# Attention block on one core: projection split four and four around the first row maxima, weights and gate product placed later

## Chip, cores, metric

The kernel runs on one core of one Trainium2 chip. The metric is the device time of one execution, in microseconds (us). TensorE is PE in the profile, VectorE DVE, ScalarE ACT, GpSimd POOL, and SyncE SP; SP only issues the DMAs here, one after the other.

## The reference, cut to what matters

The input is 2 batches of 2048 tokens with 256 features. Four residual layers follow each other: grouped attention, a feed-forward net that is applied three times, a linear attention with a gate, and the feed-forward net again. The change concerns the start of the first layer, and small pieces of the two that follow.

```python
x = x + attn_a(layernorm(x), Wq, bq, Wk, bk, Wv, bv, Wo, bo)   # 16 heads of 16, 4 KV heads
    q, k, v = x @ Wq + bq, x @ Wk + bk, x @ Wv + bv
    out = softmax(q k^T / sqrt(16)) v ;  out @ Wo + bo
x = x + ffn(layernorm(x), ...)
x = x + attn_b(layernorm(x), ...)       # gate = sigmoid(x @ Wg1 @ Wg2)
x = x + ffn(layernorm(x), ...)
```

## The kernel before

**Projection.** The 4096 tokens are 8 chunks of 512; chunks 0 to 3 are batch 0. For each chunk DVE takes moments (`moments_of`), POOL the root (`root`, a power on 4 columns), DVE scales (`scaled`), PE turns the rows (`turn_rows`), ACT copies them to `YT` (`put_row`), and PE projects: three groups of heads (`project_heads`, n = 0, 1, 2) and the values (`project_values`). Queries and keys are kept as three bf16 parts that add up to the f32 value: ACT writes the f32 value and part 0 (`high`), then comes `residue` (value minus part 0), ACT's `middle` (part 1) and `low` (part 2). `residue` and `low` are DVE's for chunks below `FREE` = 6 and POOL's for the other two. SP stores each part to DRAM (`store`: three DMAs, keys once and queries twice), and DRAM hands them back in the layout of the scores.

**Buffers of parts.** `part_a` holds two chunks, `part_b` two more; chunks 0 to 3 take turns in `part_a`, chunks 4 to 7 in `part_b`, so chunk c waits for the stores of chunk c-2 (`stored(act, 0, c - 2)`), but for chunks 4 and 5.

**Steps.** The attention is 32 steps (8 KV heads by 4 query chunks). For step s first come 64 row maxima: one bf16 matmul each on PE (`max_mm`, line 675, banks 0 to 2 of PSUM in turn) and one reduction on DVE (line 1488). When all 64 are there, DVE makes the negated maxima and signals `nm_t`; SP then issues `load_negated` (8 DMAs, line 466), and the scores of the step (lines 723 and 729) can be made with the maximum subtracted; the matmul of line 729 waits for it (`m_ld`). ACT takes the exponentials (line 1126), PE the sums with the values (line 700). In the steady state PE makes the maxima of step s+1 among the scores of step s, 16 of them (`AHEAD`) already before the step begins.

**The start.** Step 0's maxima have no scores to go beside. Before the change chunks 0 to 5 are projected, and then chunks 6 and 7 are projected in pieces between the 64 maxima (`BLOCK` = 32 maxima for each chunk). Then PE makes 16 maxima of step 1, `gate_turn` and `gate_product` (Wg1 @ Wg2, into `lvg_s`, with ACT's copies), and enters `step(0, 0)`.

**SP's queue** in order: X chunks and first weights, all 36 other weights (line 426), then the stores of the chunks with loads between them: the queries of steps 0 and 1 for the maxima (`load_queries`) after chunk 0, the keys (`load_keys`) after part 1 of chunk 3, `load_scores` of step 0 (16 coarse and 8 fine DMAs) after chunk 4 and of step 1 after chunk 6. Behind all the stores stands `load_negated(0)`, then `refill_max(0, 0)` (16 DMAs, for step 2's maxima) and the loop of the steps, which begins with `next_maxima(0, 0)`: wait for `nm_t` of step 1, `load_negated(1)`.

**Others.** POOL sets two rows of ones (`kb_ones`), copies the values of steps 0 and 1, makes residue and low of chunks 6 and 7, and adds the output bias to X (`add_bias`, line 1800, 8 instructions); DVE makes twelve small constants from the weights (lines 1450 to 1460) between chunk 5's parts and the first maximum. In `feed_forward(0)` the items n = 0, 1, ... run as a hand-written pipeline of `first(n)`, `second(n-1)`, `third(n-3)`, `fourth(n-4)` on PE, each answered by ACT. `ORDER[6]` to `ORDER[9]` are second cycles, so DVE's `update(n)` stands between PE's `first(n)` and ACT's. `global_net` of batch 1 runs at n = 8, 9, 10 and uses bank 7, as the gate product does.

Of the kernel before, what the change touches and what calls it, by code (L numbers as in the profile page):

```python
# [48 lines left out]
FREE = NCH - 2  # L49
# [21 lines left out]
def hybrid_block(nc, x, wq, bq, wk, bk, wv, bv, wo, bo, lq, lk, lv, lo, g1, g2, ln_w, ln_b,  # L71
                 c1, d1, c2, d2, c3, d3, c4, d4, e1, f1, e2, f2, e3, f3, ar,
                 ident_in, cos_in, sin_in, causal_in, head_in, diag_in, sign_in, out):
    with ExitStack() as ctx:
# [149 lines left out]
        def part(c, pt):  # L224
            return (part_a if c < CPG else part_b)[:, c % 2, pt]
# [105 lines left out]
        def buffer_of(c):  # L331
            return c // CPG * 2 + c % 2

        def stored(eng, pt, c):

            if c >= 0:
                eng.wait_ge(p_st[pt][buffer_of(c)], STORED * (c % CPG // 2 + 1))
                eng.wait_ge(k_st[pt][buffer_of(c)], 16 * (c % CPG // 2 + 1))
# [77 lines left out]
        def _(sp):  # L416
# [8 lines left out]
            for dst, src in weights:  # L425
                sp.dma_start(dst, src).then_inc(w_ld, 16)  # L426

# [52 lines left out]
            for c in range(NCH):  # L480
                store(c, 0, p_act)
                store(c, 1, p_mid)
                if c == CPG - 1:
                    for pt in range(2):
                        for p in range(2):
                            sp.wait_ge(k_st[pt][p], 16 * CPG // 2)
                    load_keys(ka, 0, 0, qa_ld)
                store(c, 2, p_low)
                if c == 0:
                    stored(sp, 0, 0)  # L490
                    stored(sp, 1, 0)
                    for s in (0, 1):
                        load_queries(qa, s, s, qa_ld)
                if c == CPG:
                    load_keys(ka, 1, 1, qa_ld)
                    stored(sp, 2, CPG - 2)
                    stored(sp, 2, CPG - 1)
                    load_scores(0, 0)
                if c == NCH - 2:
                    load_scores(1, 1)  # L500
# [106 lines left out]
        def _(pe):  # L607
# [137 lines left out]
            def gate_turn():  # L745

                pe.wait_ge(n_y, 2 * NCH)
                for kt in range(KT):
                    m = pe.transpose(ps[0:HD, 7, kt * P:(kt + 1) * P], g1_s[:, kt, :], ident[:])
                m.then_inc(w_gt, 1)  # L750

            def gate_product():

                pe.wait_ge(w_ge, 1)
                for kt in range(KT):
                    m = mm(ps[:, 7, kt * DIM:(kt + 1) * DIM], g1_t[:, kt, :], g2_s[:], start=True, stop=True)
                m.then_inc(w_gm, 1)

# [5 lines left out]
            for c in range(FREE, NCH):  # L764
                x = BLOCK * (c - FREE)
                for n in range(3):
# [4 lines left out]
                    if n < KT and c + 1 < NCH:  # L771
                        first_maxima(x, x + 1)
# [3 lines left out]
                        x += 2  # L776
# [4 lines left out]
                first_maxima(*range(x, BLOCK * (c - FREE + 1)))  # L781
            for x in range(AHEAD):
                max_mm(0, 1, x)
            pe.wait_ge(w_ld, 16 * len(weights))
            gate_turn()
            gate_product()
# [4 lines left out]
            pe.wait_ge(w_gs, KT)  # L791
# [13 lines left out]
            def feed_forward(k):  # L805
# [4 lines left out]
                def global_net(layer, b):  # L810
# [11 lines left out]
                    m.then_inc(f_g, 1)  # L822

# [56 lines left out]
                for n in range(LAST + 1):  # L880
# [176 lines left out]
        def _(act):  # L1057
# [11 lines left out]
            def high(c, n):  # L1069

                act.wait_ge(p_mm, 4 * c + n + 1)
                if n == 0:
                    if c not in (CPG, CPG + 1):
                        wait(act, p_low, c - 1)
                        stored(act, 0, c - 2)
# [4 lines left out]
            def middle(c):  # L1080
                act.wait_ge(p_res, c + 1)
                if c not in (CPG, CPG + 1):
                    stored(act, 1, c - 2)
# [18 lines left out]
            for pt in range(3):  # L1102
                for c in (NCH - 2, NCH - 1):
                    stored(act, pt, c)


            act.wait_ge(w_gt, 1)
            act.copy(g1_t[:].rearrange("p k n -> p (k n)"), ps[0:HD, 7, 0:KT * P]).then_inc(w_ge, 1)
            act.wait_ge(w_gm, 1)
            for kt in range(KT):  # L1110
                act.copy(lvg_s[:, kt, DIM:2 * DIM], ps[:, 7, kt * DIM:(kt + 1) * DIM]).then_inc(w_gs, 1)

# [35 lines left out]
            def feed_forward(k):  # L1148
                base, pairs = k * FN, k * FN // 2

                def global_net(layer, b):
# [5 lines left out]
                    if layer == 2:  # L1157
                        fn(gth[:, b:b + 1], ps[:, 7, 0:1], ACT.Tanh, bias=half_b[:, 1:2], scale=0.5).then_inc(f_ga, 1)

# [60 lines left out]
                for n in range(LAST):  # L1220
# [15 lines left out]
                    if n + 2 < NCH:  # L1236
                        put_rows(st, n + 2)

# [124 lines left out]
        def _(dve):  # L1363
# [61 lines left out]
            def low(c):  # L1425
                dve.wait_ge(p_mid, c + 1)
                if c not in (CPG, CPG + 1):
                    stored(dve, 2, c - 2)
# [20 lines left out]
            dve.wait_ge(w_ld, 16 * len(weights))  # L1449
            dve.tensor_scalar(ct_s[:, 0, :], c1_s[:, 1, :], bias[:, SG:SG + 1], -1.0, ALU.mult, ALU.mult).then_inc(c_tw, 1)  # L1450
            dve.tensor_scalar(ct_s[:, 1, :], c1_s[:, 0, :], bias[:, SG:SG + 1], None, ALU.mult).then_inc(c_tw, 1)
            dve.tensor_copy(w4_s[0:64, 0:1], last_c[0:64, 0:1])
            dve.tensor_copy(w4_s[64:P, 1:2], last_c[64:P, 0:1])
            dve.tensor_copy(c4_s[:], last_c[:, 0:1].broadcast_to((P, P))).then_inc(cols, 1)
            dve.tensor_copy(e3_s[:], last_c[0:64, 1:2].broadcast_to((64, P))).then_inc(cols, 2)
            dve.tensor_scalar(half_b[:, 0:1], bias[:, D4:D4 + 1], 0.5, None, ALU.mult)
            dve.tensor_scalar(half_b[:, 1:2], bias[:, F3:F3 + 1], 0.5, None, ALU.mult).then_inc(c_dve, 1)
            dve.memset(coup[:, 2:3], 0.1)
            dve.tensor_scalar(coup[:, 1:2], bias[:, AR:AR + 1], 0.3, None, ALU.mult)
            dve.tensor_scalar(coup[:, 3:4], bias[:, AR:AR + 1], 0.7, None, ALU.mult).then_inc(c_dve, 1)  # L1460

# [22 lines left out]
            def maxima(s, p, before=True):  # L1484
                for x in range(MAXU):
# [3 lines left out]
                    if not before and x % BLOCK == 20:  # L1489
                        put_values(FREE + x // BLOCK)  # L1490
# [10 lines left out]
            maxima(0, 0, before=False)  # L1501
            maxima(1, 1)
# [8 lines left out]
            negated_turn(STEPS - 1)  # L1511

# [267 lines left out]
        def _(pool):  # L1780
# [26 lines left out]
            def low(c):  # L1807
                pool.wait_ge(p_mid, c + 1)
                stored(pool, 2, c - 2)
# [3 lines left out]
            for c in range(NCH):  # L1813
                root(0, c)
            pool.wait_ge(n_rs, NCH)

            for pt in range(3):
                for c in (CPG - 2, CPG - 1):
                    stored(pool, pt, c)
            pool.wait_ge(p_low, CPG)  # L1820
            pool.memset(kc[FINE:FINE_M], 1.0).then_inc(kb_ones, 1)
            pool.memset(kc[HALF + FINE:HALF + FINE_M], 1.0).then_inc(kb_ones, 1)
            pool.wait_ge(kb_ones, 2)
# [5 lines left out]

            pool.wait_ge(p_val, CPG)  # L1830
            values(0, 0)
            values(1, 1)
            for c in range(FREE, NCH):
                residue(c)
                low(c)
            pool.wait_ge(w_ld, 16 * len(weights))
            pool.wait_ge(nm_t, 1)
            for c in range(NCH):
                add_bias(c)
            pool.wait_ge(p_val, NCH)  # L1840
            pool.wait_ge(n_bo, NCH)
# [4 lines left out]

            for c in range(NCH):
# [138 lines left out]
```

## Time and profile before

| | us |
|---|---|
| median of 3 runs | 2129.47 (2126.69 to 2131.73) |
| profiled execution | 2132.38 |
| its span, first to last instruction | 2130.6 |
| PE busy in the span | 2007.4 (94%) |
| DVE busy in the span | 1824.8 (86%) |
| ACT busy in the span | 1488.5 (70%) |

The span is what a trace covers; the execution's own time is a little longer. A busy share is an average over stages that have different limits, so the stages are read one by one: a row of a timeline gives the start, the length, the engine, the line, what is written from what, the count, and in brackets the idle time before it and who ended it.

### The profile page before, as it was taken

What the parts mean: (1) busy time and instruction counts of PE and PEld (TensorE: products, weight loads), DVE (VectorE), ACT (ScalarE), POOL (GpSimd) and SP (SyncE); (2) the same over time, 40 slices, a digit from 0 to 9 for tenths busy, and PEclk for the clock granted to TensorE, in tenths of its full rate; (3) what the DMA queues carried; (4) which work ended last, traced back from release to release, by engine and by line L of the source; (5) the groups of instructions that cost most, each with busy time, mean ns of one, the idle gap of its engine ahead of it and who ended that gap; (6) DMA issues with size and microseconds to landing.
All of it is one profiled execution on the core that took longest, in us unless ns stands there. A gap on an engine that the chain in (4) does not pass through costs nothing.

```text
span 2130.6 us, 47788 instructions
## 1 busy us (share of the span) xinstructions
PE 2007.4 (94%) x13990; PEld 819.3 (38%) x13990; DVE 1824.8 (86%) x3396; ACT 1488.5 (70%) x2939; POOL 178.9 (8%) x298
## 2 busy tenths in 40 slices
PE   7689999999999999999999999989997799998995
PEld 4323333333333333333333333334433466665432
DVE  6789999999999999999999999945449977777358
ACT  4428888888888888888888888854457554444757
POOL 1250000000000000000000000001005211002001
PEclk9769999999999999999999999999998899998998
DMA  6421122122112112112212212222000000000002
GB/s 163 135 75 43 44 64 64 43 58 70 43 53 71 46 47 73 50 45 69 56 43 67 60 42 65 52 88 87 1 1 1 1 1 1 1 0 1 1 1 80
DMA packets 110232, 101.34 MB, mean 48 GB/s; under 512 B 52240, under 2 KB 91424, under 8 KB 110096
## 3 DMA queue, kind: packets, MB, share of 16 engines
q1 hardware_dynamic: 110096, 99.92, 17.6%
q14 instruction: 99, 0.81, 0.1%
q8 instruction: 37, 0.61, 0.1%
HBM read 78.79 MB, written 20.77 MB: 47 GB/s over the span
## 4 chain that ended last, share of the span: by engine, by line
PE 82%; DVE 7%; ACT 4%; issue 3%; SPq 3%; DMA 1%; ACTq 0%; DVEq 0%; POOL 0%; POOLq 0%
PE ps L700 22%; PE ps L675 15%; PE ps L723 10%; PE ps L729 10%; PE ps L840 6%; PE ps L849 3%; PE ps L938 2%; PE ps L947 2%; PE ps L986 2%; PE ps L689 2%; ACT YT L1126 2%; PE ps L967 1%; PE ps L1017 1%; DVE X L1607 1%; SPq L426 1%
## 5 line engine op out<-in xcount | busy, mean ns | idle before, releaser
L1488 DVE TENSOR_REDUCE mx<-ps 128x1 f32<-128x512 f32 x2048 | 1279.8, 683 | 21.1 <-PE ps L675 16.5
L1126 ACT ACTIVATE YT<-ps 128x512 f32<-128x512 f32 x2048 | 1058.2, 605 | 253.0 <-PE ps L729 253.0
L700 PE MATMUL ps<-YT,work 128*32 128x512 f32 x4096 | 546.2, 605 | 0.0
L675 PE MATMUL ps<-work 64*128 64x512 bf16 x2048 | 460.7, 389 | 16.0 <-DVE mx L1488 13.3
L723 PE MATMUL ps<-work 64*128 64x512 bf16 x2048 | 402.5, 378 | 1.7
L729 PE MATMUL ps<-work 34*128 34x512 bf16 x2048 | 398.9, 378 | 0.0
L675 PEld LDWEIGHTS ps<-work 64*128 64x128 bf16 x2048 | 144.6, 93 | 620.8 <-DVE mx L1488 547.0
L723 PEld LDWEIGHTS ps<-work 64*128 64x128 bf16 x2048 | 162.0, 94 | 106.4 <-ACT YT L1126 32.0
L700 PEld LDWEIGHTS ps<-YT,work 128*32 128x32 f32 x4096 | 80.7, 108 | 122.9 <-issue 87.2
L729 PEld LDWEIGHTS ps<-work 34*128 34x128 bf16 x2048 | 101.2, 94 | 49.2 <-issue 1.3
L1827 POOL COPY work<-vals 128x512 f32 (+1 forms) x32 | 19.6, 613 | 1191.9 <-PE ps L700 1191.8
L849 PE MATMUL ps<-work,c_s 128*128 128x512 f32 x192 | 97.1, 630 | 14.5 <-ACT work L1177 12.1
L1688 DVE TENSOR_TENSOR work<-ps,causal 128x512 f32<-128x512 f32 x128 | 81.7, 681 | 22.0 <-PE ps L967 22.0
L840 PE MATMUL ps<-YT,c_s 128*128 128x512 f32 x128 | 62.3, 632 | 5.0 <-ACT vals L1172 2.8
L938 PE MATMUL ps<-lqk_s,work 128*128 128x512 f32 x128 | 63.6, 620 | 3.4 <-DVE work L1706 2.2
L840 PE MATMUL ps<-YT,ct_s 128*128 128x512 f32 x128 | 60.9, 619 | 4.3 <-issue 4.3
L947 PE MATMUL ps<-lvg_s,work 128*128 128x512 f32 x128 | 61.7, 605 | 3.1 <-ACT YT L1062 3.1
L1306 ACT ACTIVATE work<-ps 128x128 f32<-128x128 f32 x64 | 14.2, 274 | 69.2 <-PE ps L947 69.2
L849 PEld LDWEIGHTS ps<-work,c_s 128*128 128x128 f32 x192 | 36.0, 196 | 65.8 <-issue 45.5
L1326 ACT ACTIVATE work<-ps,bias 128x128 f32<-128x128 f32 x64 | 25.8, 454 | 38.1 <-PE ps L1007 38.1
L1672 DVE TENSOR_TENSOR work<-work,cos_s 128x256 f32<-128x256 f32 x64 | 27.0, 422 | 29.2 <-ACT work L1298 29.1
L620 PE MATMUL ps<-ident,xn 128*128 128x128 f32 x256 | 37.3, 292 | 15.6 <-DVE xn L1394 10.8
(178 smaller groups left out, 1809.6 us busy)
## 6 DMA issues: line engine op xcount, KB each, us to landing
work<-k_scr SPq DMA_DIRECT2D x640, 64.0 KB, 2.2
work<-q_scr SPq DMA_DIRECT2D x640, 32.0 KB, 1.8
o_scr<-o_sb SPq DMA_DIRECT2D x32, 256.0 KB, 2.2
X<-in_L_attn_a_x_dram SPq DMA_DIRECT2D x8, 512.0 KB, 7.4
work<-negt SPq DMA_DIRECT2D x256, 1.0 KB
work<-o_scr SPq DMA_DIRECT2D x16, 256.0 KB
work<-inv_scr SPq DMA_DIRECT2D x16, 256.0 KB
out_dram<-X SPq DMA_DIRECT2D x8, 512.0 KB, 2.9
```

The lines of the kernel that those rows point to most:

```text
L675: mm(ps[:, bank_of[x], :], qa[rows, p, jp, qt * P:(qt + 1) * P], ka[rows, p, kc_ * CH:(kc_ + 1) * CH], start=True, stop=True).then_inc(a_m ...
L689: m = mm(ps[:, last_bank(c, h), (t % 2) * DIM:(t % 2 + 1) * DIM], a_in[:, c % 2, kt, t * P:(t + 1) * P], wo_s[:, kt, :], start=kt == 0, st ...
L700: m = mm(ps[32 * j:32 * j + 32, 7, :], vst[:, p, t, :], prob(GROUP * t + j), start=t == 0, stop=t == KTILES - 1)
L723: mm(ps[:, S_BANK + (u + g) % S_RING, :], kb[rows, p, t * P:(t + 1) * P], qb[rows, p, jp, :], start=True, stop=False)
L729: mm(ps[:, S_BANK + (u + g) % S_RING, :], kc[rows, p, t * P:(t + 1) * P], qc[rows, p, jp, :], start=False, stop=True).then_inc(qk_mm, 1)
L840: m = mm(ps[:, b_ + mt, :], w[:, kt, mt * P:(mt + 1) * P], YT[:, kt, ch(c)], start=kt == 0, stop=kt == KT - 1)
L849: m = mm(ps[:, 2, :], c2_s[:, kt, :], h1[:, n % 2, kt, :], start=kt == 0, stop=kt == KT - 1)
L938: m = mm(ps[:, 0, :], y_st8[:, p, kt, :], lqk_s[:, kt, :], start=kt == 0, stop=kt == KT - 1)
L947: m = mm(ps[:, 1, :], y_st8[:, p, kt, :], lvg_s[:, kt, :], start=kt == 0, stop=kt == KT - 1)
L1126: fn(prob(u), ps[:, S_BANK + u % S_RING, :], ACT.Exp, scale=HD ** -0.5).then_inc(exp_ok, 1)
L1488: dve.tensor_reduce(mx[:, p, at_:at_ + 1], ps[:, bank_of[x], :], AX_X, ALU.max).then_inc(a_max, 1)
L1688: dve.tensor_tensor(e_m[:, i], ps[:, 3 + i, :].rearrange("p (a n) -> p a n", n=P), causal[:].rearrange("p (a n) -> p a n", a=1).broadcast_ ...
```

## The change

- `FREE` = `CPG` = 4 and so `BLOCK` = 16: chunks 0 to 3 are projected first, then chunks 4 to 7 in pieces between step 0's maxima, 16 maxima for each chunk, two ahead of each piece; the turns of rows have no maxima of their own any more. Residue and low of chunks 4 to 7 are POOL's.
- The four part buffers are shared: chunk c waits for the stores of chunk c-4.
- DVE: `scaled(0, 6)` and `moments_of(0, 7)` come after maximum 4 of step 0, `scaled(0, 7)` after maximum 20; POOL's `root(0, 7)` comes after `residue(4)` and `low(4)`. The values of a chunk are taken after the third maximum of the next block.
- SP: the 36 weights come after `refill_max(0, 0)`; the queries of steps 0 and 1 after chunks 1 and 2; the keys of step 0 after all of chunk 3; step 1's after chunk 4; both `load_scores` after chunk 5, behind a wait for all parts of chunks 2 to 5; `load_negated(0)` between parts 1 and 2 of chunk 7.
- POOL: the ones and the copies of the values after all residues; `add_bias` behind the loop of the value copies, so in step 30.
- DVE's twelve constants come after the last negated maxima.
- `gate_turn` and `gate_product` move into `feed_forward(0)`, to n = 6 and n = 7, behind the other work of the item; PE then waits for ACT's copies of the product.

```diff
-FREE = NCH - 2
+FREE = CPG
 BLOCK = MAXU // (NCH - FREE)
...
-            return (part_a if c < CPG else part_b)[:, c % 2, pt]
+            return (part_a, part_b)[c // 2 % 2][:, c % 2, pt]
...
         def buffer_of(c):
-            return c // CPG * 2 + c % 2
+            return c % CPG
...
-            for dst, src in weights:
-                sp.dma_start(dst, src).then_inc(w_ld, 16)
...
             for c in range(NCH):
                 store(c, 0, p_act)
                 store(c, 1, p_mid)
+                if c == NCH - 1:
+                    sp.wait_ge(nm_t, 1)
+                    load_negated(0)
+                store(c, 2, p_low)
+                if c in (1, 2):
+                    for pt in range(2):
+                        stored(sp, pt, 0)
+                    load_queries(qa, c - 1, c - 1, qa_ld)
                 if c == CPG - 1:
...
                     load_keys(ka, 0, 0, qa_ld)
...
                 if c == CPG:
                     load_keys(ka, 1, 1, qa_ld)
...
+                if c == CPG + 1:
+                    for pt in range(3):
+                        for c4 in range(2, CPG + 2):
+                            stored(sp, pt, c4)
+                    for s in (0, 1):
+                        load_scores(s, s)
...
-            sp.wait_ge(nm_t, 1)
-            load_negated(0)
             refill_max(0, 0)
+            for dst, src in weights:
+                sp.dma_start(dst, src).then_inc(w_ld, 16)
...
-                        first_maxima(x, x + 1)
                         if n == 0:
                             pe.wait_ge(n_xn, c + 2)
                         turn_rows(0, c + 1, n)
-                        x += 2
...
+                    if k == 0 and n == GLOBAL_AT[1] - 2:
+                        gate_turn()
+                    if k == 0 and n == GLOBAL_AT[1] - 1:
+                        gate_product()
+                        pe.wait_ge(w_gs, KT)
...
+                    if not before and x >= BLOCK and x % BLOCK == 2:
+                        put_values(FREE + x // BLOCK - 1)
+                    if not before and x == 4:
+                        scaled(0, NCH - 2)
+                        dve.wait_ge(x_ld[NCH - 1], 16)
+                        moments_of(0, NCH - 1)
+                    if not before and x == BLOCK + 4:
+                        scaled(0, NCH - 1)
...
+            for c in range(FREE, NCH):
+                residue(c)
+                low(c)
+                if c == FREE:
+                    root(0, NCH - 1)
```

## Rows read from the trace of the kernel before

**Rows 1.** The page's chain that ended last, share by engine
```profile
PE 82%; DVE 7%; ACT 4%; issue 3%; SPq 3%; DMA 1%; ACTq 0%; DVEq 0%; POOL 0%; POOLq 0%
```

**Rows 2.** Windows: stretch and length, busy by engine, granted clock, DMA share, GB/s
```profile
77.20:134.10 56.90, 42.80 (x130) 14.16 (x130) 50.94 (x80) 13.07 (x17) 20.58 (x8) 0.74 0.44 126
190.60:1391.80 1201.20, 1199.85 (x9520) 413.17 (x9520) 1191.52 (x2020) 994.01 (x1933) 18.39 (x30) 1.00 0.21 56
1527.60:1565.90 38.30, 38.26 (x97) 15.57 (x98) 20.44 (x19) 16.96 (x29) 0.00 (x0) 0.96 0.03 1
```

**Rows 3.** Timeline of PE: gate product, first scores that need negated maxima
```profile
144.09 2.07 PE L756 MATMUL ps<-g_s,g_t 16*128 16x256 f32 x4 [0.53 <-ACT g_t L1108]
...
148.01 0.66 PE L729 MATMUL ps<-work 34*128 34x512 bf16 x2
```

**Rows 4.** Timeline of PE, projection before and among the maxima
```profile
32.92 3.60 PE L641 MATMUL ps<-YT,wq_s 128*128 128x512 f32 x8
...
58.51 6.32 PE L641 MATMUL ps<-YT,wq_s 128*128 128x512 f32 x8 [5.99 <-ACT work L1078]
...
98.34 1.13 PE L641 MATMUL ps<-YT,wkk_s 128*128 128x512 f32 x2
```

**Rows 5.** Timeline of DVE: a chunk's parts, moments, a constant, the first maxima
```profile
31.81 1.76 DVE L1423 TENSOR_TENSOR work<-work 128x1536 f32<-128x1536 f32 x1 [0.56 <-ACT work L1078]
...
35.10 1.76 DVE L1429 TENSOR_TENSOR work<-work 128x1536 bf16<-128x1536 f32 x1 [1.20 <-ACT work L1084]
...
65.69 1.38 DVE L1394 TENSOR_SCALAR xn<-X,moments,norm 128x256 f32<-128x256 f32 x4
66.98 1.39 DVE L1378 BATCH_NORM_STATS2 bn<-X 128x6 f32<-128x256 f32 x4
...
83.91 3.68 DVE L1451 TENSOR_SCALAR ct_s<-c_s,bias 128x256 f32<-128x256 f32 x1
...
88.92 2.46 DVE L1488 TENSOR_REDUCE mx<-ps 128x1 f32<-128x512 f32 x4
```

**Rows 6.** Timeline of ACT: part 1 of chunk 1
```profile
33.60 1.47 ACT L1084 CAST work<-work 128x1536 bf16<-128x1536 f32 x1 [1.82 <-DVE work L1423]
```

**Rows 7.** Timeline of SP: a store's two query DMAs, eight coarse loads, negated maxima of steps 0 and 1
```profile
56.79 1.27 SPq L477 DMA_DIRECT2D q_scr<-work  x2
...
90.97 3.66 SPq L441 DMA_DIRECT2D work<-k_scr  x8
...
137.12 5.35 SPq L466 DMA_DIRECT2D work<-negt  x8
...
183.72 5.20 SPq L466 DMA_DIRECT2D work<-negt  x8
```

**Rows 8.** DMA issues up to 200 us: count, size, issue to landing
```profile
work<-k_scr SPq DMA_DIRECT2D x56, 64.0 KB, 2.2
```

**Rows 9.** Timeline of POOL: a root, a residue, the bias adds
```profile
70.56 1.01 POOL L1792 TENSOR_TENSOR norm<-var,mhalf 128x4 f32<-128x4 f32 x1
...
102.23 3.09 POOL L1805 TENSOR_TENSOR work<-work,part_b 128x1536 f32<-128x1536 f32 x1 [13.56 <-ACT part_b L1078]
...
137.16 18.45 POOL L1800 TENSOR_TENSOR X<-X,bo_s 128x1024 f32<-128x1024 f32 x8 [6.84 <-issue]
```

**Rows 10.** SP's waits up to 200 us: total, times, longest
```profile
SPq L337 <- DMA q_scr<-part_b: 2.3, 1, 2.3
```

**Rows 11.** End of the maxima: DVE's reciprocal of the sums
```profile
1393.75 3.31 DVE L1515 RECIPROCAL den<-den 112x512 f32<-112x512 f32 x1
```

**Rows 12.** SP writes that reciprocal out
```profile
1401.75 0.46 SPq L563 DMA_DIRECT2D inv_scr<-den  x1
```

**Rows 13.** Feed-forward: PE at items 6 and 8
```profile
1527.64 5.37 PE L840 MATMUL ps<-YT,ct_s 128*128 128x512 f32 x8 [2.17 <-issue]
...
1542.07 0.60 PE L817 MATMUL ps<-gm,e_s 128*128 128x1 f32 x4
```

**Rows 14.** Feed-forward: ACT's last work of item 7
```profile
1545.55 1.51 ACT L1203 ACTIVATE work<-work,cb,coup 128x512 f32<-128x512 f32 x2
```

More of the change, by code:

```diff
@@ L822, in global_net, with gate_turn, gate_product @@
                     m.then_inc(f_g, 1)
+                def gate_turn():
+                    pe.wait_ge(f_ga, 3)
+                    for kt in range(KT):
+                        m = pe.transpose(ps[0:HD, 7, kt * P:(kt + 1) * P], g1_s[:, kt, :], ident[:])
+                    m.then_inc(w_gt, 1)
+                def gate_product():
+                    pe.wait_ge(w_ge, 1)
+                    for kt in range(KT):
+                        m = mm(ps[:, 7, kt * DIM:(kt + 1) * DIM], g1_t[:, kt, :], g2_s[:], start=True, stop=True)
+                    m.then_inc(w_gm, 1)
                 def first(n):
@@ L1101, in _ @@
                 middle(c)
[L1102 to L1111, printed above, removed]
             def collect(s, i, p):
@@ L1158, in global_net, with gate_turn, gate_product @@
                         fn(gth[:, b:b + 1], ps[:, 7, 0:1], ACT.Tanh, bias=half_b[:, 1:2], scale=0.5).then_inc(f_ga, 1)
+                def gate_turn():
+                    act.wait_ge(w_gt, 1)
+                    act.copy(g1_t[:].rearrange("p k n -> p (k n)"), ps[0:HD, 7, 0:KT * P]).then_inc(w_ge, 1)
+                def gate_product():
+                    act.wait_ge(w_gm, 1)
+                    for kt in range(KT):
+                        act.copy(lvg_s[:, kt, DIM:2 * DIM], ps[:, 7, kt * DIM:(kt + 1) * DIM]).then_inc(w_gs, 1)
                 def first(n):
@@ L1237, in feed_forward @@
                         put_rows(st, n + 2)
+                    if k == 0 and n == GLOBAL_AT[1] - 2:
+                        gate_turn()
+                    if k == 0 and n == GLOBAL_AT[1] - 1:
+                        gate_product()
                 coupled(LAST + 1)
@@ L1511, in _ @@
             negated_turn(STEPS - 1)
+            constants()
             dve.wait_ge(den_ld, 16)
@@ L1808, in low @@
                 pool.wait_ge(p_mid, c + 1)
-                stored(pool, 2, c - 2)
+                stored(pool, 2, c - CPG)
                 pool.tensor_tensor(part(c, 2), qkf(c), part(c, 1), ALU.subtract).then_inc(p_low, 1)
             pool.wait_ge(consts, 4)
-            for c in range(NCH):
+            for c in range(NCH - 1):
                 root(0, c)
[L1815 to L1823, printed above, removed]
+            pool.wait_ge(n_rs, NCH - 1)
             def values(s, p):
@@ L1828, in values @@
                                  vals[:, kv_of(s)].rearrange("p t d -> p (t d)")).then_inc(v_st, 1)
+            for c in range(FREE, NCH):
[3 more added lines that the diff above has]
+                    root(0, NCH - 1)
+            for pt in range(3):
+                for c in range(2, CPG + 2):
+                    stored(pool, pt, c)
+            pool.wait_ge(p_low, NCH)
+            pool.memset(kc[FINE:FINE_M], 1.0).then_inc(kb_ones, 1)
+            pool.memset(kc[HALF + FINE:HALF + FINE_M], 1.0).then_inc(kb_ones, 1)
+            pool.wait_ge(kb_ones, 2)
             pool.wait_ge(p_val, CPG)
@@ L1832, in _ @@
             values(1, 1)
[L1833 to L1839, printed above, removed]
             pool.wait_ge(p_val, NCH)
-            pool.wait_ge(n_bo, NCH)
             with pool.Fori(1, STEPS // 2) as i:
@@ L1844, in _ @@
                 values(2 * i + 1, 1)
+            pool.wait_ge(w_ld, 16 * len(weights))
+            for c in range(NCH):
+                add_bias(c)
+            pool.wait_ge(n_bo, NCH)
             for c in range(NCH):
```

70 lines of the change are left out of this document (21 added, 49 removed).

## The prediction, made blind

> **What bounds the kernel now.** I read the chain that ended last first: PE holds 82% of it [rows 1]. The windows say where that is true. In the 30 steps from 190.6 to 1391.8 us PE is busy 1199.85 of 1201.20 us at full granted clock [rows 2], and nothing in the change touches a step's inside. In the start, 77.2 to 134.1, no engine is full (PE 42.8 of 56.9 us, DVE 50.9) and the granted clock is 0.74 [rows 2]; there order and waits decide. In the feed-forward stretch from 1527.6 to 1565.9 PE is again never idle (38.26 of 38.30) [rows 2], so whatever is put there is paid for. So three questions: when do the steps begin, is a later step held up, and what does the gate cost in its new place? My mark for the beginning is the first matmul that needs negated maxima, at 148.01 [rows 3]; all that follows hangs on it.
>
> **Start, up to the first maximum.** Chunks 0 to 3 have four part buffers, so the waits for stores between chunks go (5.99 us before one chunk [rows 4]); by the projection row 32.92 [rows 4] chunks then follow each other at under 9 us. A residue takes 1.76, part 1 1.47, low 1.76 [rows 5, 6]; chunk 3's low ends near 53. SP, free of the 36 weights, becomes the last to finish: from chunk 1's part 1 (near 35.1) it issues, one after the other, stores at 3 issues of 0.63 = 1.9 each [rows 7] and loads at 3.7 for eight [rows 7]: two stores, queries, three stores, queries, three stores, keys = 8 x 1.9 + 3 x 3.9 = 27, so until 62.2. The last key DMA lands 2.2 us after its issue [rows 8]: first maximum at **64.0**. DVE begins its maxima at 88.92 today [rows 5], so the first maximum is 25 us earlier. That is the gain on paper.
>
> **Chunks 4 to 7 among 64 maxima.** A piece of projection is 1.13 us at full clock [rows 4], with its two maxima 1.38; eight pieces and two turns make 12.2 us for a block, against 16 reductions of 0.615 (2.46 for four [rows 5]), so PE sets the pace. Block 4 starts cold: PE has stood idle for 16 us, and a row after 5.99 us of idleness takes 6.32 against 3.60 [rows 4], +2.7. DVE then makes a detour after maximum 4: `scaled` 1.38 and moments 1.39 + 0.38 [rows 5], 3.1 us, of which PE feels 1.4 after its run-ahead of three banks. Block 4: 64.0 + 12.2 + 2.7 + 1.4 = 80.3. Chunk 4's last head is out at 79.1; POOL's residue takes 3.09 [rows 9], part 1 1.47, POOL's low 3.1, waits between 0.2: 87.0, and only then comes `root(0, 7)`, 1.01 and 0.3 before it [rows 9]: 88.3. DVE asks for it after maximum 20, at 84.7. It waits 3.6 us, then scales for 1.4. Queued behind that wait are all further reductions; PE, three maxima ahead, stands 3.3 us and works at half clock after it, +2. Block 5 ends at 80.3 + 12.2 + 5.3 = 97.8; chunk 5's low, 7.8 us behind its last head (96.6), at **104.4**. Blocks 6 and 7 need 12.2 and 11.0: the 64 maxima end at 122, 12 us before today (134.1), and `nm_t` would allow the negated load at 125.
>
> **SP is not ready for it.** Behind chunk 5's low SP issues its store (1.9), waits for its landing (2.3 [rows 10]; one such wait is all there is to read), and then issues both `load_scores`: 48 DMAs at 0.46 [rows 7] = 22.2. Then come the stores of chunk 6 (5.8) and two of chunk 7 (3.9), and only then `load_negated(0)`, 5.35 [rows 7]. Sum: 104.4 + 1.9 + 2.3 + 22.2 + 5.8 + 3.9 + 5.35 = 145.9; landing after the last issue 1.6 to 2.4, I take 1.9: the first matmul with negated maxima at **147.8**. Today it is 148.01, where the negated load ended at 142.5 [rows 7] and the gate product (2.07 and its copies) stood in the way [rows 3]. So 0.2 us is gained. 25 us earlier at the first maximum, 12 at the last, and none at the steps: SP's in-order queue eats it. Bounds: with neither DVE's stalls nor the cold pieces behind them the mark is 7 us earlier (141); with landings of 3 us and another half-clock stretch 5 us later (153).
>
> **Step 1.** `load_negated(1)` stands behind store 7,2 (1.9), its landing (2.4), `refill_max` (7.4) and 36 weights, issued today from 13.6 to 36.7, 23.0 us for the lot; together 34.7 after the first negated load's end, at 180.6. It is wanted 183.72 - 148.01 = 35.7 after the mark [rows 3, 7], at 183.5. Cost 0, margin 2.9 us; if the weights' issue is slower by more than that, each further us delays step 1 and all behind it. Range 0 to +3.
>
> **End of the steps.** `add_bias`, 18.45 us [rows 9], moves into step 30, beside reductions from PSUM; that step begins some 30 us before DVE's last maximum, so the adds are over about 9 us before it. The constants, twelve small instructions of DVE, stand before the reciprocal of the sums, which ends at 1397.1 today [rows 11] and is fetched by SP at 1401.75 [rows 12], as SP is busy until then. 256 columns scaled cost 0.35 (1.38 for four [rows 5]); the twelve come to 2.1 by that, so 4.6 us of cover hide them. Today one of them took 3.68 [rows 5] while POOL worked. The Trainium skill (SBUF — State Buffer, Who interferes with whom) gives the reason as an exclusive lock: the second of VectorE in a two-port mode and GpSimd to issue is blocked for the other's whole instruction. By it the constants would cost the 7.5 us that they take today (81.4 to 88.92 [rows 5]) if the bias adds met them, and 2.9 would come out behind the cover; the trace has the adds finished first, so the sum keeps 0.
>
> **The gate in the feed-forward.** Two turns on PE at n = 6 cost about 0.35. At n = 7 the product's four matmuls take 1.0 at full clock (2.07 at half [rows 3]), issued 0.35 later than where item 8 begins today (1542.07 [rows 13]): done at 1543.4. Then PE waits for ACT's copies, and ACT gets to them after its own item 7, whose last work ends at 1547.1 today [rows 14] (0.35 later: 1547.4); copies 0.65, signal 0.3: PE goes on at 1548.3. Item 8 is 6.2 us late. After 4.9 us of idleness PE's granted clock will be the lower level: 2.17 us of idleness turned 3.60 into 5.37 [rows 13], 5.99 us into 6.32 [rows 4], so +1.8 to +2.7, I take 1.9. PE is the full engine from here to 1565.9 [rows 2] and all later items hang on it, so nothing is won back: **+8.1** (6.2 to 9.0). Its old place gives nothing back, since the start is SP's now.
>
> **Sum.** -0.2 + 0 + 0 + 8.1 = +7.9 against the profiled execution's 2132.38 (span 2130.6), that is 2140.3; the median of the runs is 2129.47, 2.9 lower, so 2137.4.
>
> **Rivals.**
> - A, faster: SP reaches `load_negated(0)` when `nm_t` allows it. For this the 48 score loads, or the stores behind them, must be issued far faster than 0.46 each. Then the mark is at 125 + 5.35 + 1.9 + 1 = 133 to 134, 14 us gained, 8.1 lost: 2123.6. It decides from 12.4 us saved in the queue upwards. Against it: every issue row reads 0.46, loaded or not [rows 7]. 0.12.
> - B, the stalls of DVE and PE in blocks 4 and 5 don't come, the mark is at 141.5: -6.5 + 8.1 = +1.6, 2131.1. For it: a root that comes in time. Against it: 5 us of waits that follow from the order in POOL's queue. 0.17.
> - C, the gate costs nothing in the feed-forward, because ACT's answer comes in time or later waits take up the delay: -0.2, 2129.3. Against it: PE 38.26 of 38.30 us busy [rows 2]. 0.09.
> - D, the weights hold up step 1 (their 23.0 us become 29 beside other loads): +3 more, 2140.5, up to 2145. 0.14.
> - Forecast: 0.48.
>
> **Numbers.** A difference under 0.2% (4.3 us) is about what a measurement of this kernel can't tell from none. Faster is A: 0.12. Same is B and C: 0.26. Slower is the forecast and D: 0.62. The forecast's own range is 2133.5 to 2142; the range that is to hold 8 times in 10 goes down to C (2129.3) and up into D, 2129 to 2144.5, and leaves A and D's far end out.
>
> **What would show it.** First maximum near 64 and DVE's reductions of step 0 over near 122; DVE idle some 3.6 us for POOL's root before `scaled(0, 7)`; SP without a gap from about 108 to 146, issuing the negated load with no wait for `nm_t`; PE idle for it, and line 729 first at 148. Then `load_negated(1)` waiting for DVE, not behind weights. In the feed-forward one PE gap of 4 to 5 us released by ACT's copy into `lvg_s`, and half the granted clock after it. The forecast is wrong if line 729 starts before 144, if SP waits for `nm_t`, or if that gap is under 2 us.

## The result, and the profile after

The changed kernel takes 2147.72 us (median of 4 runs, 2142.39 to 2150.51) against 2130.6 for the kernel before, run beside it (4 runs, 2126.69 to 2132.53): ratio 1.0085, 95% interval 1.0071 to 1.0099. Slower was forecast, but by 7.9 us and not by 17; 2147.72 lies above the whole range. The profiled execution is the fastest of the four: 2142.39 us, span 2140.6, against the 2140.3 that the sum gave for it. That near agreement is an accident, as the stages show.

**The start.** PE's timeline, kernel after (start, length, engine, line, what, and the idle time before with who ended it):

```profile
63.54 0.61 PE L675 MATMUL ps<-work 64*128 64x512 bf16 x2 [16.57 <-DMA work<-k_scr]
...
134.22 0.61 PE L675 MATMUL ps<-work 64*128 64x512 bf16 x2 [4.57 <-POOL work L1838]
134.60 0.65 PE L723 MATMUL ps<-work 64*128 64x512 bf16 x2
148.03 0.60 PE L729 MATMUL ps<-work 34*128 34x512 bf16 x2 [12.78 <-DMA work<-negt]
```

SP's timeline, the same kernel (`load_scores` of steps 0 and 1, the negated maxima of step 0, the last weight, the negated maxima of step 1):

```profile
108.79 3.57 SPq L430 DMA_DIRECT2D work<-q_scr  x8
...
131.72 0.56 SPq L470 DMA_DIRECT2D k_scr<-part_b  x1
...
141.56 5.38 SPq L463 DMA_DIRECT2D work<-negt  x8
...
182.07 0.91 SPq L524 DMA_DIRECT2D bias<-in_L_attn_b_ln_b_dram  x2
183.34 5.39 SPq L463 DMA_DIRECT2D work<-negt  x8
```

The first maximum is at 63.54, 25 us earlier than before. DVE's negated maxima of step 0 are ready at 123.44, but SP, busy without a break from 108.79, issues them at 141.56. PE stands idle for 12.78 us, and the mark is at 148.03 against 148.01 [rows 3]. Of the 25 us won at the first maximum 13.4 were left at the negated maxima (136.81 before), and none at the mark.

**The steps.** DVE's timeline, kernel after: the negated maxima that end the maxima of a step. The first five gaps come to 200.69 us, 40.1 each; then every second one is late. The last line is the last step's.

```profile
183.11 0.20 DVE L1480 STREAM_TRANSPOSE negt<-negq 128x32 bf16<-128x32 bf16 x1
...
383.80 0.20 DVE L1480 STREAM_TRANSPOSE negt<-negq 128x32 bf16<-128x32 bf16 x1
425.23 0.20 DVE L1480 STREAM_TRANSPOSE negt<-negq 128x32 bf16<-128x32 bf16 x1
465.39 0.20 DVE L1480 STREAM_TRANSPOSE negt<-negq 128x32 bf16<-128x32 bf16 x1
506.93 0.20 DVE L1480 STREAM_TRANSPOSE negt<-negq 128x32 bf16<-128x32 bf16 x1
...
1404.05 0.21 DVE L1480 STREAM_TRANSPOSE negt<-negq 128x32 bf16<-128x32 bf16 x1
```

The same instruction, kernel before:

```profile
183.50 0.20 DVE L1482 STREAM_TRANSPOSE negt<-negq 128x32 bf16<-128x32 bf16 x1
...
384.19 0.20 DVE L1482 STREAM_TRANSPOSE negt<-negq 128x32 bf16<-128x32 bf16 x1
424.84 0.20 DVE L1482 STREAM_TRANSPOSE negt<-negq 128x32 bf16<-128x32 bf16 x1
464.99 0.20 DVE L1482 STREAM_TRANSPOSE negt<-negq 128x32 bf16<-128x32 bf16 x1
...
1393.62 0.21 DVE L1482 STREAM_TRANSPOSE negt<-negq 128x32 bf16<-128x32 bf16 x1
```

These 30 steps took 1210.12 us and now take 1220.94: **+10.8**, in a stretch in which the diff touches nothing. The late steps are the 13 in which ACT turns its own loop of two steps (`act.Fori(2, STEPS // 2)`; a turn is the jump from the loop's end back to its head): 40.6 to 40.9 us before, 41.4 to 41.7 after. The last step is shorter than the others, 38.1 us without a turn, and comes to 38.5 before and 39.7 after. ACT's timeline at the first turn, kernel after, shows it:

```profile
389.37 2.06 ACT L1112 ACTIVATE YT<-ps 128x512 f32<-128x512 f32 x4 [0.42 <-PE ps L729]
393.30 2.06 ACT L1112 ACTIVATE YT<-ps 128x512 f32<-128x512 f32 x4 [1.87 <-issue]
```

and the kernel before:

```profile
389.75 2.07 ACT L1126 ACTIVATE YT<-ps 128x512 f32<-128x512 f32 x4 [0.42 <-PE ps L729]
392.91 2.06 ACT L1126 ACTIVATE YT<-ps 128x512 f32<-128x512 f32 x4 [1.09 <-PE ps L729]
```

In the groups ahead of it ACT waits 0.42 to 0.58 us. Here it waits 1.09 before and 1.87 after, in the second case for nothing that the profile names ("issue"). ACT's waits from 190 to 1391.8 us, kernel after, have a line that has no counterpart before:

```profile
ACT YT L1112 <- issue: 17.6, 9, 2.0
```

**The gate in the feed-forward.** PE's timeline, kernel after:

```profile
1533.32 5.37 PE L833 MATMUL ps<-YT,ct_s 128*128 128x512 f32 x8 [2.17 <-issue]
...
1547.87 1.12 PE L814 MATMUL ps<-g_s,g_t 16*128 16x256 f32 x4
1553.44 1.01 PE L796 MATMUL ps<-gm,e_s 128*128 128x1 f32 x4 [4.45 <-ACT lvg_s L1153]
1554.32 5.42 PE L833 MATMUL ps<-YT,ct_s 128*128 128x512 f32 x8
...
1562.65 3.70 PE L833 MATMUL ps<-YT,ct_s 128*128 128x512 f32 x8
```

Items 8 and 9, kernel before:

```profile
1542.54 3.68 PE L840 MATMUL ps<-YT,ct_s 128*128 128x512 f32 x8
...
1549.13 3.70 PE L840 MATMUL ps<-YT,ct_s 128*128 128x512 f32 x8
```

PE waits 4.45 us for ACT's copies, and the next item begins at the lower granted clock: 5.42 for what takes 3.68, with a mean of 0.66 from 1553.44 to 1560.00, where item 8 had 1.00 before. From item 6 to item 9 it is 29.33 us against 21.49 (1527.64 [rows 13] to 1549.13): **+7.84**.

**The rest.** From the last negated maxima to item 6 of the feed-forward the profiled run is 4.75 us shorter than before (129.27 against 134.02), and from item 9 to the end of the span 3.52 (577.95 against 581.47). In the kernels of the first two groups below the same stretches take 129.9 to 133.6 and 578.8 to 585.1 us, in no order that follows an edit, so I count both as scatter. The spans' +10.0 is then -0.4 (start, read at step 1's negated maxima) + 10.8 - 4.75 + 7.84 - 3.5, and without the scatter 10.8 + 7.8 = 18.6 stands against the +17.1 of the medians.

### The profile page after: what moved, and what is told of

Same layout as the page of the kernel before. It is cut to its first block, busy times and chain, and to the rows that moved or that the text cites. A ratio compares the mean times of both kernels' runs of the same rounds, so it can differ in the third digit from the quotient of the medians.

```text
span 2140.6 us, 47800 instructions
## 1 busy us (share of the span) xinstructions
PE 1997.0 (93%) x13990; PEld 815.5 (38%) x13990; DVE 1811.2 (85%) x3392; ACT 1488.4 (70%) x2939; POOL 192.9 (9%) x302
## 4 chain that ended last, share of the span: by engine, by line
PE 81%; DVE 6%; ACT 4%; issue 4%; SPq 3%; DMA 1%; POOL 1%; ACTq 0%; DVEq 0%; POOLq 0%
PE ps L700 22%; PE ps L675 14%; PE ps L723 10%; PE ps L729 10%; PE ps L833 6%; PE ps L842 3%; PE ps L936 2%; PE ps L945 2%; ACT YT L1112 2%; PE ps L984 1%; PE ps L689 1%; PE ps L965 1%; PE ps L1015 1%; DVE X L1613 1%; PE ps L620 1%
## 5 line engine op out<-in xcount | busy, mean ns | idle before, releaser
L842 PE MATMUL ps<-work,c_s 128*128 128x512 f32 x192 | 97.6, 633 | 15.1 <-ACT work L1172 12.7
L1163 ACT ACTIVATE work<-vals,bias 128x512 f32<-128x512 f32 x32 | 21.3, 714 | 47.1 <-DVE vals L1584 47.1
L620 PE MATMUL ps<-ident,xn 128*128 128x128 f32 x256 | 37.6, 292 | 15.1 <-DVE xn L1393 10.3
```

The costliest lines, as they stand in the source:

```text
L620: m = pe.transpose(ps[:, turn_bank(st, c, kt), t * P:(t + 1) * P], xn[:, c % 2, t, kt * P:(kt + 1) * P], ident[:])
L842: m = mm(ps[:, 2, :], c2_s[:, kt, :], h1[:, n % 2, kt, :], start=kt == 0, stop=kt == KT - 1)
```

## The experiments

Each kernel is described by three values: the mark, the 30 steps (from step 1's negated maxima to step 31's), and the time from item 6 to item 9. Experiments of one group ran beside the same runs of the kernel before (median 2129.36 of 19 runs in the first group, 2129.32 of 19 in the second; 2129.8, one run, in the third).

### First group: one cost taken out of the changed kernel at a time

**Nine instructions put back on ACT.** ACT's code ahead of its loop is 419 instructions in the compiled kernel before and 410 in the changed one; the loop's body is 294 in both. (These three are counts of the compiled programs; no trace shows them.) The edit adds 18 waits on a semaphore that has long been reached ahead of the first step. Two waits become one instruction: the page of the profile counts 47809 instructions against 47800.

```diff
+            for _ in range(18):
+                act.wait_ge(w0_ld, 16 * len(first_weights))
```

> The changed kernel with 18 waits on a semaphore that is long full put ahead of ACT's loop of steps; they come to 9 instructions, so that the loop begins at the same place of ACT's program as in the kernel before (419 instructions ahead of it, against 410 in the changed kernel). Theory 'place': the turn of ACT's loop costs more in the changed kernel only because the loop stands elsewhere; then the 30 steps from the negated maxima of step 1 to those of step 31 take 1210 us again and not 1221, and the span falls by about 7 to 11 us. Theory 'traffic': the turn is longer because of what else runs in the steps (DMAs, POOL); then the 30 steps keep 1221 us. Start (line 729 first at 148.0) and the gate's gap (4.5 us) stay in both.

Measured: 2139.19 us (8 runs, 2134.19 to 2145.95), ratio 1.0049 [1.0033, 1.0066]. The 30 steps take 1210.08 us, as before the change; ACT's wait at the first turn is back at 1.07. So the steps' loss is no work and no wait of the change; it hangs on where ACT's loop lies in its program. The medians fell by 8.5 us, as expected, but the two profiled spans by only 1.4 (2140.6 to 2139.2), since the stretches behind the steps were 8.7 us longer in this one; what is compared here is the stage.

**ACT's loop written out.**

```diff
-            with act.Fori(2, STEPS // 2) as i:
+            for i in range(2, STEPS // 2):
```

> The changed kernel with ACT's 28 looped steps written out, so that ACT has no loop in the attention. If ACT's turn holds up PE, every second step loses its extra 1.3 us and the 30 steps take 30 x 40.15 = 1205 us, 16 us less than the changed kernel and 6 less than the kernel before, so about 2126 us. If the loss sits in another engine's loop, they keep 1221 us.

Measured: 2133.89 us (10 runs, 2127.83 to 2137.97), ratio 1.0023 [1.0009, 1.0037]. Every step but the last (38.09) takes 40.1 to 40.2, the 30 of them 1202.46. So the kernel before should pay for its turns too, which the second group shows. The expected 2126 fits the changed kernel's profiled run, its shortest, less 16; between the medians the time fell by 13.8 us, where the steps give 18.5 and a later mark (149.69) takes back 1.7.

**SP's queue in another order.** Step 1's score loads go behind the stores of chunk 7 and step 0's negated maxima, and the weights behind the first two turns of SP's steps.

```diff
-                    for s in (0, 1):
-                        load_scores(s, s)
+                    load_scores(0, 0)
...
+            load_scores(1, 1)
...
-            for dst, src in weights:
-                sp.dma_start(dst, src).then_inc(w_ld, 16)
-            with sp.Fori(0, STEPS // 2 - 2) as i:
+            for p in range(2):
+                next_maxima(p, p)
+                refill_max(p + 1, 1 - p)
+                leave(p, p)
+                refill(p, p)
+                for dst, src in weights[p * len(weights) // 2:(p + 1) * len(weights) // 2]:
+                    sp.dma_start(dst, src).then_inc(w_ld, 16)
+            with sp.Fori(1, STEPS // 2 - 2) as i:
```

> The changed kernel with SP's order alone altered: the second load of scores behind the negated maxima of step 0, and the weights in two halves behind steps 0 and 1. Theory 'queue' (the prediction's): line 729 of step 0 starts as soon as POOL's last copy allows, near 136.5 and not at 148.0, and all after it is 11 us earlier. Rival: PE is held by something else as well (values, rows of ones, another transfer), and the mark moves by less than 3 us.

Measured: 2138.58 us (6 runs, 2135.29 to 2142.49), ratio 1.0049 [1.0032, 1.0067]. PE's timeline:

```profile
137.25 0.61 PE L734 MATMUL ps<-work 34*128 34x512 bf16 x2 [1.70 <-DMA work<-negt]
```

The mark is 10.8 us earlier, and PE's wait of 12.78 us is down to 1.70. The start's gain was there, and SP's order was what held it. The 30 steps still take 1220.44.

**The gate product in another gap.** It goes behind the last step, where PE waits for the sums to come back for the output projection; ACT copies it there in the last step, for which its last two steps stand behind its loop, so that it turns once less (ACT's part and the removed functions are not shown).

```diff
@@ PE, output projection
+                    for kt in range(KT):
+                        m = pe.transpose(ps[0:HD, 2, kt * P:(kt + 1) * P], g1_s[:, kt, :], ident[:])
+                    m.then_inc(w_gt, 1)
+                    pe.wait_ge(w_ge, 1)
+                    for kt in range(KT):
+                        m = mm(ps[:, 2, kt * DIM:(kt + 1) * DIM], g1_t[:, kt, :], g2_s[:], start=True, stop=True)
+                    m.then_inc(w_gm, 1)
+                if c == 1:
+                    pe.wait_ge(w_gs, KT)
@@ PE, feed-forward
-                    if k == 0 and n == GLOBAL_AT[1] - 2:
-                        gate_turn()
-                    if k == 0 and n == GLOBAL_AT[1] - 1:
-                        gate_product()
-                        pe.wait_ge(w_gs, KT)
```

> The changed kernel with the gate's turns and product moved out of the feed-forward into step 31, ahead of the first output projection, where PE waits 6 to 7 us for a DMA (bank 2 in place of bank 7); for this ACT's last two steps stand outside its loop. Theory 'gap': item 8 of the feed-forward comes 5.7 us after item 7's end no more, and 7.9 us of the stretch from item 6 to item 9 are gone; nothing is added in step 31. Rival: the delay was hidden by later waits, and the span changes by less than 3 us.

Measured: 2140.27 us (4 runs, 2139.86 to 2143.59), ratio 1.0059 [1.0036, 1.0082]. PE's timeline at items 8 and 9:

```profile
1552.22 0.61 PE L805 MATMUL ps<-gm,e_s 128*128 128x1 f32 x4
1552.69 3.68 PE L828 MATMUL ps<-YT,ct_s 128*128 128x512 f32 x8
...
1559.28 3.70 PE L828 MATMUL ps<-YT,ct_s 128*128 128x512 f32 x8
```

No gap, no half clock, and 21.49 us from item 6 to item 9, to the hundredth what it was before. The output projection begins 22.74 us after the last negated maxima, where kernels without the product there have 21.1 to 22.6: what the new place costs, 1.7 us at most, is not told from the scatter.

### Second group: all of it together, and the turn alone

**All three edits** on the changed kernel, with ACT's loop written out:

> All three costs taken out of the changed kernel: the first loads for negated scores of the two parts divided (step 1's scores load and the weights moved behind step 0's negated parts), the gate product back in the gap after the last steps, ScalarE's loop over the steps written out. If the three are separate and each is worth what its own run showed: first matmul of the scores of step 0 at about 137.3 us (148.03 in the changed kernel), 30 steps of 40.15 us after the first two (1202.5 us, 1220.94 in the changed kernel), item 6 to item 9 of the last feed-forward 21.5 us (29.3). That is 10.8 + 18.5 + 7.8 less about 4 for the tail, so 2106 to 2115 us, against some 2130 for the kernel before: ratio 0.989 to 0.993. If they overlap (a later wait takes the place of the gain at the start, as one theory has it), no better than 2120.

Measured: **2110.97 us** (4 runs, 2110.88 to 2112.37), ratio 0.9917 [0.99, 0.9933]: faster than both kernels, 36.8 us below the changed one, and in the middle of the expected range. The mark is at 137.93, the 30 steps take 1202.52, items 6 to 9 take 21.49. What holds the mark now is partly POOL (PE's timeline):

```profile
135.45 0.61 PE L680 MATMUL ps<-work 64*128 64x512 bf16 x2 [4.56 <-POOL work L1826]
135.83 0.66 PE L737 MATMUL ps<-work 64*128 64x512 bf16 x2
137.93 0.61 PE L743 MATMUL ps<-work 34*128 34x512 bf16 x2 [1.44 <-DMA work<-negt]
```

**The kernel before with ACT's loop written out** (the same one-line edit):

> The kernel before with nothing changed but ScalarE's loop over the steps written out. If each turn of that loop costs the kernel before 0.5 to 0.8 us: 30 steps take about 1202.5 us in place of 1210.1, and the time falls by 7.6 us, to about 2122 (ratio 0.9964). If the turn costs the kernel before nothing, and only the changed kernel pays for it: 1210 us and no difference.

Measured: 2120.9 us (10 runs, 2113.63 to 2126.67), ratio 0.9956 [0.9941, 0.9971]; the 30 steps take 1202.47.

**The kernel before with 7 and with 23 instructions more** ahead of ACT's loop (the padding of the first experiment, with 14 and 46 waits):

> The kernel before with 7 instructions (14 satisfied waits, paired) more on ScalarE ahead of its loop over the steps: 426 in place of 419. If the turn's price goes by where the loop lies modulo 16 instructions, this is the place of the changed kernel (410) and the 30 steps take about 1221 us, the time rises by some 11 us to 2141. If the price goes by the place in another measure, or by the length of code alone, the steps stay near 1210 us and the time within 0.2% of before.

> The kernel before with 23 instructions more on ScalarE ahead of its loop over the steps: 442 in place of 419, the changed kernel's place (410) modulo 32. If the turn's price goes by the place modulo 32 (or 16) instructions: 30 steps of about 1221 us in sum and some 2141 us. Otherwise near 1210 us and within 0.2% of before.

Measured (two waits are one instruction again: 14 waits for 7, 46 for 23): with 7, 2134.0 us (10 runs, 2131.06 to 2135.82), ratio 1.0023 [1.0013, 1.0032], 30 steps 1212.13. With 23, 2153.89 us (4 runs, 2147.35 to 2154.43), ratio 1.0106 [1.0084, 1.0128], 30 steps 1234.16: 46 waits that are over at once, and +24.6 us. That sum was in no expectation. Neither 16 nor 32 instructions is the measure, as neither kernel has the changed kernel's 1221. ACT's timeline at the turn, with 23:

```profile
391.54 0.60 ACT L1129 ACTIVATE YT<-ps 128x512 f32<-128x512 f32 x1 [1.26 <-PE ps L729]
393.64 1.57 ACT L1129 ACTIVATE YT<-ps 128x512 f32<-128x512 f32 x3 [1.50 <-issue]
```

ACT gets one of its four exponentials through and stands again: as if the loop's head lay at the end of one block of code, and the next had to come too.

### Third group: what is the measure?

The profile counts packets of instructions. This is its part on DMA queues from 190 to 1380 us (packets, MB, share), kernel after:

```profile
q14 instruction: 73, 0.60, 0.2%
```

and with ACT's loop written out, in the changed kernel:

```profile
q14 instruction: 25, 0.20, 0.1%
```

Only ACT's program differs, so queue 14 brings ACT's code. Writing the loop out makes the program longer and the fetched code less: the loop fetches its code again at its turns. But the kernel before fetches as much as the changed one:

```profile
q14 instruction: 73, 0.60, 0.2%
```

and the kernel before with 23 instructions more fetches 68 packets. So what a turn costs is not told by how much code it fetches. One packet is 0.60 MB / 73 = 8.2 KB. The Trainium skill (Runtime: NRT & Kernel Launch, Instruction fetch mechanics) says that a taken branch to a target outside the resident window forces a fetch before execution goes on, that most engines hold 32 KiB, and that code comes in 16 KiB blocks of 256 instructions. By the size of an instruction that follows from it (16 KiB / 256 = 64 B) I estimate a packet of 8.2 KB at 128 instructions, so two periods were open, 128 and 256. Four kernels, each the kernel before with padding (two waits for each instruction) and run once, tell them apart:

> The kernel before with 128 instructions more on ScalarE ahead of its loop over the steps (547 in place of 419), the size of one packet of the instruction queue (8 KB at 64 B an instruction). If the turn's price goes by where the loop lies within such a block: the 30 steps take 1210 us as before, with turns of 40.6 to 40.9 us. If it goes by the length of the code or by an address in another measure: some other sum. The padding itself delays the first exponentials, so the start is later; the steps are what is read.

> The kernel before with 151 instructions more on ScalarE ahead of its loop (570), that is 128 more than in the kernel with 23 more. If the place within a block of 128 decides: 30 steps of about 1234 us, every second step 42.1 to 43.9 us. Otherwise not.

> The kernel before with 119 instructions more on ScalarE ahead of its loop (538), which is 128 more than the 410 of the changed kernel. If the place within a block of 128 decides: the 30 steps take about 1221 us, as in the changed kernel, with turns of 41.4 to 41.7 us. If the changed kernel's turns come from anything else that it changed: 1210 us.

> The kernel before with 55 instructions more on ScalarE ahead of its loop (474), the changed kernel's place modulo 64 but not modulo 128. If the place within a block of 128 decides, a sum between those seen (1210 to 1234 us) but not that of the changed kernel, as the loop's first instruction then lies 64 further into its block; if a block of 64 decides, about 1221 us.

Measured, beside the others (instructions ahead of ACT's loop; its place modulo 128):

| kernel | ahead | modulo 128 | 30 steps, us |
|---|---|---|---|
| after | 410 | 26 | 1220.94 |
| before + 119 | 538 | 26 | 1221.22 |
| before | 419 | 35 | 1210.12 |
| after + 9 | 419 | 35 | 1210.08 |
| before + 128 | 547 | 35 | 1210.77 |
| before + 7 | 426 | 42 | 1212.13 |
| before + 23 | 442 | 58 | 1234.16 |
| before + 151 | 570 | 58 | 1233.73 |
| before + 55 | 474 | 90 | 1202.73 |

Three pairs agree within 0.7 us at a distance of 128 instructions, and 410 and 474, at a distance of 64, do not: 128 is the measure. That is half the block that the Trainium skill states; here the measurement decides. The other queue of instructions does move packets of the size that it states, 0.61 MB / 37 = 16.5 KB (the page of the profile, kernel before):

```profile
q8 instruction: 37, 0.61, 0.1%
```

The last row of the table is the kernel before with its loop as it is and 55 instructions of padding: no turn costs anything, and queue 14 brings hardly any code. Its expectation missed, since both of its theories asked for at least 1210 us. It also answers a rival of the loop written out. That edit takes 1821 instructions from the page's count (47800 to 45979), and the gain could be theirs; but here they all run, and the steps take 1202.73. Its instruction queue, 190 to 1380 us, and ACT at the turn:

```profile
q14 instruction: 10, 0.08, 0.0%
```

```profile
391.39 2.06 ACT L1129 ACTIVATE YT<-ps 128x512 f32<-128x512 f32 x4 [0.42 <-PE ps L729]
393.88 2.06 ACT L1129 ACTIVATE YT<-ps 128x512 f32<-128x512 f32 x4 [0.43 <-PE ps L729]
```

A body of 294 instructions lies in three blocks of 128 if it begins at one of the first 91 of a block, and in four otherwise. The costly places, 410 to 442, fit into the last 37 of one block, and 474 into the next. That four blocks are held (the 32 KiB that the Trainium skill states), so that three and the next one ahead of them stay resident and four do not, fits every row; where the blocks' borders lie was not measured, and this reading is argued, not shown. The whole time of the padded kernels says less: 2139.43, 2165.42, 2146.24 and 2126.89 us in the order of the four expectations, one run each, and 119 or more instructions of padding also delay step 1 (its negated maxima are at 187 to 192).

## Why the prediction was right in its sign and wrong in its size

**The terms against all timed kernels.** Start (mark), steps and gate, each against the kernel before's profile (148.01, 1210.12, 21.49), beside the difference of medians:

| kernel | start | steps | gate | sum | medians |
|---|---|---|---|---|---|
| after | 0.0 | +10.8 | +7.8 | +18.7 | +17.1 |
| after, 9 instructions back | +0.5 | 0.0 | +7.4 | +7.9 | +9.8 |
| after, ACT's loop written out | +1.7 | -7.7 | +7.7 | +1.7 | +4.5 |
| after, SP's queue | -10.8 | +10.3 | +7.9 | +7.5 | +9.2 |
| after, gate elsewhere | +0.8 | +10.0 | 0.0 | +10.7 | +10.9 |
| all three | -10.1 | -7.6 | 0.0 | -17.7 | -18.4 |
| before, ACT's loop written out | -2.7 | -7.7 | 0.0 | -10.3 | -8.4 |
| before + 7 | -0.6 | +2.0 | 0.0 | +1.4 | +4.7 |
| before + 23 | -1.5 | +24.0 | 0.0 | +22.5 | +24.6 |

The terms are read in the profiled run of each kernel, the medians are of all its runs. Three terms account for nine kernels within 3.3 us. The prediction had sizes for two of them, the start and the gate, and none for the steps.

**What failed.** "In the 30 steps ... PE is busy 1199.85 of 1201.20 us at full granted clock, and nothing in the change touches a step's inside." True, and it settled the wrong thing: work that is not touched was taken to keep its time. The change took nine instructions off ACT's code ahead of the loop and so moved the loop within its program, and every turn of it became dearer. Cost: 10.8 us, where the sum had no term. It is shown from both sides: nine instructions put back give 1210.08 us, and the kernel before with 119 more, 128 away from the changed kernel's place, gives 1221.22. No bound covered it; the range ended at 2144.5, and with this term it would have been 2140.3 + 10.8 = 2151.1 for the profiled execution, or 2148.2 for the median (2147.72 measured). The busy share hid it as well, since PE's rows grow longer when it is held: in the kernel after, at the first turn, two pairs of matmuls of line 723 take 0.88 where pairs in the groups ahead of the turn take 0.38 (PE's timeline). And in the kernel before the turn's loss of 0.5 to 0.8 us was in the trace to be read, every second step at 40.6 to 40.9 beside 40.15, and ACT's 1.09 among 0.42s. An even beat with an odd step in it was not looked for.

```profile
393.41 0.39 PE L675 MATMUL ps<-work 64*128 64x512 bf16 x2
393.95 0.88 PE L723 MATMUL ps<-work 64*128 64x512 bf16 x2 [0.16 <-ACT YT L1112]
394.45 0.60 PE L729 MATMUL ps<-work 34*128 34x512 bf16 x2
```

**The start, right.** First maximum 64.0 forecast, 63.54 measured; chunk 5's low 104.4, 103.83; the mark 147.8, 148.03. The sum of SP's queue held almost row for row (load of the negated maxima forecast to end near 145.9, measured 146.94), and the reordering of SP's queue shows that it was the cause. Inside it one step was wrong without harm: DVE did not wait for POOL's root. PE's granted clock was 0.67 over block 4, as pieces went back to 2.07 us each after PE had stood 1.50 us for DVE's detour, so the block took 20.0 us in place of 16.3, DVE came later to its second detour than the forecast had it, and POOL had the root by then (a window of 64.10 to 84.10, busy by engine and then the granted clock; DVE's timeline; POOL's):

```profile
64.10:84.10 20.00, 18.29 (x55) 8.23 (x53) 13.08 (x28) 5.54 (x9) 3.09 (x1) 0.67 0.05 16
```

```profile
88.56 0.69 DVE L1486 TENSOR_REDUCE mx<-ps 128x1 f32<-128x512 f32 x1 [0.21 <-PE ps L675]
89.22 1.38 DVE L1393 TENSOR_SCALAR xn<-X,moments,norm 128x256 f32<-128x256 f32 x4
```

```profile
88.18 1.01 POOL L1798 TENSOR_TENSOR norm<-var,mhalf 128x4 f32<-128x4 f32 x1
```

Block 5 began at 84.1 in place of 80.3 and had no stall for the root, so it ended at 97.6 (97.8 forecast): the two errors cancelled, and that the start came out so close is luck in part.

**Step 1, right, and close.** The weights took 23.9 us from 159.09 (23.0 forecast), and SP was free at 182.98. DVE's negated maxima were done at 183.31 and their load followed at 183.34, so of the margin of 2.9 us 0.3 was left. Rival D didn't come.

**The gate, right.** +8.1 forecast, +7.84 measured; the gap 4.9, measured 4.45; the lower clock behind it cost 1.7 (1.9 forecast). The experiment that moves it elsewhere takes all of it away, so rival C is out.

**End of the steps, right.** The bias adds ran from 1375.11 to 1393.7, the twelve constants from 1404.19 to 1405.5 (1.3 us, 2.1 forecast), ahead of the reciprocal, which SP stored at 1412.20. The rule of the Trainium skill weighed there (SBUF — State Buffer, Who interferes with whom) found no case here: the adds were over before the constants began.

**The rivals.** A (SP free in time) needed 12.4 us out of the queue; as the change stands SP had none to give, and when the queue is reordered the mark goes to 137.25, 3 to 4 us behind A's 133 to 134. The reason given against A was wider than its rows: only the loads for scores read 0.46 an issue, a store's queries read 0.63 and the negated loads 0.67 [rows 7]; the 48 score loads took 22.9 us, as forecast within 0.7. B's condition came true in part (no stall for the root), but the mark did not move, as block 4 was slower than forecast.

**Still open.** Of the four runs of the changed kernel the profiled one is the shortest, by up to 8.1 us; what the others spend it on no trace here shows. Why a place costs 0.5 to 0.8, 1.3 to 1.6 or 1.8 to 3.8 us a turn, for about the same number of packets, is not worked out, nor why with 7 instructions more the steps between turns take 40.27 in place of 40.15.

## What to carry to other kernels

Before a steady loop is costed at nothing, write down the start of every step, before and after: a delay that shows in one step of two or four can be a loop's turn on some engine, and its price can change with any edit ahead of it. Whoever shortens a chain of work must walk the in-order queue that carries its result, to see whether the queue is there in time; here negated maxima that were ready 13 us earlier waited 18 us for SP, behind score loads of which half were for a later step. And a small product that needs another engine's answer belongs where the engine waits anyway, not where it is full.

## What was unexpected of the hardware

A loop of 294 instructions on ACT costs between nothing and 3.8 us a turn here, by where its first instruction lies modulo 128: 30 steps took 1202.7, 1210, 1212, 1221 or 1234 us with the same work. At the costly places code is fetched again at the turns (68 to 74 packets of 8.2 KB against 10), and 23 instructions that only wait for what is long over made the kernel 1% slower, while 55 of them made it no slower (2126.89 us against 2129.8, one run each). And the kernel before lost 7.7 us to it all along.
